# Value bias added to the turned attention output, value copies on ScalarE, gate folding on GpSimd, third batch's norm ahead of the first division

## The reference, cut to what matters

```python
def _L0_attn_ref(x, Wq, bq, Wk, bk, Wv, bv, Wo, bo):
    ...
    V = proj(Wv, bv)
    ...
    att = jax.nn.softmax(scores, axis=-1)
    y = jnp.einsum('bhqk,bhkd->bhqd', att, V)
    y = y.transpose(0, 2, 1, 3).reshape(B, T, H)
    return jnp.einsum('bth,oh->bto', y, Wo) + bo
...
mod = (_silu(L0_c) @ L0_wmod).reshape(L0_c.shape[0], 6, 1, -1)
sa, ca, ga, sb, cb, gb = (mod[:, 0], mod[:, 1], mod[:, 2], mod[:, 3], mod[:, 4], mod[:, 5])
ga = (2 * (ga >= 0) - 1) * jnp.maximum(jnp.abs(ga), 0.25)
gb = (2 * (gb >= 0) - 1) * jnp.maximum(jnp.abs(gb), 0.25)
h = _layernorm(x, axis=-1) * (1 + ca) + sa
x = x + ga * _L0_attn_ref(h, ...)
h = _layernorm(x, axis=-1) * (1 + cb) + sb
x = x + gb * _L0_ffn_ref(h, ...)
```

## Time and profile before

| | us |
|---|---|
| median of 3 runs | 386.95 (384.18 to 386.96) |
| profiled execution, device time | 386.66 |
| its span, first to last instruction | 384.7 |
| TensorE busy | 335.2 (87%) |
| VectorE busy | 282.9 (74%) |
| ScalarE busy | 256.4 (67%) |
| GpSimd busy | 145.7 (38%) |

### The profile page before, as it was taken

How to read it: one execution, slowest core, us unless ns; L and a number is a source line. 1 busy time by engine, 2 the same in 40 slices (tenths; PEclk the granted TensorE clock), 3 DMA queues, 4 the chain that set the end, 5 groups by cost and what they waited for, 6 DMA issues and landing times.

```text
span 384.7 us, 7186 instructions
## 1 busy us (share of the span) xinstructions
PE 335.2 (87%) x2636; PEld 153.8 (40%) x2636; DVE 282.9 (74%) x585; ACT 256.4 (67%) x276; POOL 145.7 (38%) x179
## 2 busy tenths in 40 slices
PE   3759688989899889898999999898998889779996
PEld 3425254546455334334654434335552323141123
DVE  5879968877899986874799877973598467933334
ACT  8580463534289778855488788736678788849980
POOL 6249327601407234941208136722150246212500
PEclk9956899999999999999999999999999999989999
DMA  7335133300026255500144355510060557515540
GB/s 262 113 68 84 26 60 52 47 5 0 4 55 96 79 136 153 164 13 2 29 92 76 86 141 137 132 30 21 13 84 0 136 137 137 107 49 135 158 131 29
DMA packets 27115, 31.53 MB, mean 82 GB/s; under 512 B 6780, under 2 KB 17788, under 8 KB 27068
## 3 DMA queue, kind: packets, MB, share of 16 engines
q1 hardware_dynamic: 23372, 28.57, 32.3%
q0 software_dynamic: 3456, 2.39, 3.0%
q10 hardware_dynamic: 252, 0.11, 0.2%
HBM read 3.57 MB, written 1.05 MB: 12 GB/s over the span
## 4 chain that ended last, share of the span: by engine, by line
PE 51%; DVE 27%; issue 7%; DMA 7%; ACT 4%; SPq 2%; POOL 1%; DVEq 0%; ACTq 0%; POOLq 0%
PE misc L1315 17%; PE big L1315 17%; PE acc L1315 15%; DVE mx L1055 8%; DMA dense<-tp 4%; ACT ring L804 3%; PE misc L1337 2%; DMA block<-qk_turned 1%; DVE xn L995 1%; DMA gm<-wT 1%; SPq L502 1%; DVE second L1140 1%; DVE stats L970 1%; SPq L527 1%; DMA xs<-in_x 1%
## 5 line engine op out<-in xcount | busy, mean ns | idle before, releaser
L804 ACT ACTIVATE ring<-big 128x1024 f32<-128x1024 f32 (+1 forms) x201 | 195.5, 1021 | 79.3 <-PE big L1315 78.4
L1055 DVE TENSOR_REDUCE mx<-misc 128x1 f32<-128x512 f32 (+7 forms) x155 | 87.3, 588 | 23.7 <-PE misc L1315 21.7
L1315 PE MATMUL acc<-ring,cb 128*32 128x512 f32 x512 | 67.8, 604 | 3.1 <-ACT ring L804 1.6
L1315 PE MATMUL big<-tstack,w1s 128*128 128x512 bf16 x192 | 55.0, 381 | 4.0 <-ACT ring L804 3.8
L1315 PE MATMUL misc<-dense,block 128*128 128x320 bf16 (+7 forms) x170 | 43.4, 316 | 11.4 <-DVE mx L1055 10.4
L1315 PE MATMUL big<-dense,block 128*128 128x512 bf16 (+7 forms) x256 | 51.1, 306 | 0.4 <-ACT ring L804 0.2
L1175 DVE SCALAR_TENSOR_TENSOR gm<-acc,cb,gm 128x512 f32<-128x512 f32 (+1 forms) x41 | 30.0, 733 | 25.6 <-PE acc L1315 19.4
L1315 PEld LDWEIGHTS misc<-dense,block 128*128 128x128 bf16 x170 | 20.9, 149 | 51.2 <-DVE mx L1055 41.3
L456 POOL DMA_DIRECT2D block<-qk_turned x66 | 39.3, 601 | 2.5 <-DMA tstack<-tp 1.3
L1315 PE MATMUL acc<-ring,vals 128*32 128x256 f32 (+7 forms) x512 | 37.9, 412 | 0.0
L1315 PEld LDWEIGHTS big<-dense,block 128*128 128x128 bf16 x256 | 28.7, 149 | 22.5 <-ACT ring L804 9.7
(11 more groups left out here) (163 smaller groups left out, 462.8 us busy)
## 6 DMA issues: line engine op xcount, KB each, us to landing
gm<-wT SPq DMA_DIRECT2D x64, 256.0 KB
dense<-qk SPq DMA_DIRECT2D x42, 64.0 KB
tstack<-tp SPq DMA_DIRECT2D x18, 128.0 KB, 4.6
block<-qk_turned POOLq DMA_DIRECT2D x66, 32.0 KB, 3.5
xs<-in_x SPq DMA_DIRECT2D x4, 256.0 KB, 7.8
ca<-in_pack_a SPq DMA_DIRECT2D x1, 769.0 KB, 7.1
out<-lg SPq DMA_DIRECT2D x3, 256.0 KB, 2.3
dense<-tp SPq DMA_DIRECT2D x6, 128.0 KB, 10.4
```

The costliest lines, as they stand in the source:

```text
L804: act.activation(dst, src, func, scale=scale).then_inc(s["ring_read"], 1)
L1055: dve.tensor_reduce(mx[:, g, k:k + n, blk], src, AX.X, ALU.max).then_inc(s["misc_read"], 1)
L1315: return pe.matmul(dst, lhsT, rhs, start=start, stop=stop)
```

## The change

The value bias leaves `values`: it becomes a column of pack_b and is added by `turn_output` when `yT` is copied (a `tensor_scalar` in place of a copy, with a wait for pack_b). pack_a is 128 columns narrower, pack_b one wider. The copies into `vals` for batches 1, 2 and 3 go to ScalarE: for batch 1 behind `take_sums`, for 2 and 3 ahead of the fifth expert unit; VectorE waits there until the bank is read. `fold_gates` goes to GpSimd, behind `stack_q(1)`, with two-operation `tensor_scalar`s and one product per gate. `normalise` of batch 2 stands ahead of that wait and of the first `divide`.

```diff
--- before.py
+++ after.py
@@ -64,9 +64,9 @@
     return out, at
 
 
-A_COLS, A_W = columns(("we", P), ("wd", P), ("wv", D), ("cos", T), ("sin", T), ("be", 1), ("bd", 1), ("bv", D))
+A_COLS, A_W = columns(("we", P), ("wd", P), ("wv", D), ("cos", T), ("sin", T), ("be", 1), ("bd", 1))
 C_COLS, C_W = columns(("cT", NB), ("wmod", 6 * D))
-B_COLS, B_W = columns(("woT", D), ("bout", D), ("wm", D), ("bm", 1), ("emb", D), ("w2", NEP * HR),
+B_COLS, B_W = columns(("woT", D), ("bout", D), ("wm", D), ("bm", 1), ("bv", 1), ("emb", D), ("w2", NEP * HR),
                       ("b2", 2), ("wof", 2 * D), ("bof", D), ("sum", HR), ("first", NE), ("keep", 2))
 
 
@@ -191,7 +191,6 @@
     return uses, banks, previous, [last[1], last[3]]
 
 
-FOLD_AT = [13, 16]
 OPENING, OPENING_BANK, OPENING_PREVIOUS, LAST_IN_ACC = opening()
 
 
@@ -361,7 +360,7 @@
         s = {n: ctx.enter_context(nc.semaphore(n)) for n in (
             "a_loaded", "b_loaded", "c_loaded", "x0_loaded", "x1_loaded", "x_loaded", "w1_loaded", "ones_loaded",
             "nought_ready", "zeroed", "cleared", "k_block_cleared", "spare_cleared", "mod_linked", "marks", "tabled", "shapes_ready", "exp_ready", "abs_ready", "sil_ready", "mod_ready",
-            "gates_filled", "setup_link", "modb_ready", "w1_ready", "summed", "rows_cleared", "tokens_one",
+            "gates_filled", "gates_folded", "setup_link", "modb_ready", "w1_ready", "summed", "rows_cleared", "tokens_one",
             "var_ready", "pow_ready", "xn_ready", "out_gates", "w1_rounded", "w1_less", "expert_gates", "xb_ready", "x1b_ready",
             "misc_filled", "misc_read", "ring_filled", "ring_read", "consumed", "acc_read",
             "qk_ready", "qk_turned", "k_dense_stacked", "q_block0_stacked", "q_block1_stacked", "q_dense_stacked", "k_block_stacked", "nm_ready",
@@ -654,6 +653,14 @@
                 else:
                     pool.tensor_tensor(w1f, rounded, w1f, ALU.add).then_inc(s["w1_less"], 1)
 
+            def fold_gates(k):
+
+                pool.wait_ge(s["abs_ready"], 2 * k + 2)
+                pool.tensor_scalar(graw[k], graw[k], 0.0, 0.5, ALU.is_ge, ALU.subtract).then_inc(s["gates_folded"], 1)
+                pool.tensor_scalar(gabs[k], gabs[k], 0.25, 2.0, ALU.max, ALU.mult).then_inc(s["gates_folded"], 1)
+                pool.wait_ge(s["gates_folded"], 3 * k + 2)
+                pool.tensor_tensor(gate[:, k, :, :], graw[k], gabs[k], ALU.mult).then_inc(s["gates_folded"], 1)
+
             def fold_out(b, here=None):
 
                 if here:
@@ -718,6 +725,8 @@
             cut_weights(0)
             pool.wait_ge(s["spare_cleared"], 2)
             stack_q(1)
+            for k in range(2):
+                fold_gates(k)
             pool.wait_ge(s["qk_turned"], 6)
             stack_k(1)
             k_blocks(1, K_BLOCKS)
@@ -725,7 +734,7 @@
             pool.wait_ge(s["x0_loaded"], 16)
             pool.wait_ge(s["x1_loaded"], 16)
             pool.wait_ge(s["x_loaded"], 16 * (NB - 2))
-            pool.wait_ge(s["gates_filled"], 2)
+            pool.wait_ge(s["gates_folded"], 6)
             fold_out(0)
             pool.wait_ge(s["xb_ready"], 1)
             cut_weights(1)
@@ -827,6 +836,16 @@
                     wait_consumed(act, phase, NSS * g + NSS - 1)
                     act.copy(sums[g][:, :], acc[:, g, :]).then_inc(s["acc_read"], 1)
 
+            def values(here, b, turn=None):
+                wait_softmax_over(act, b, turn)
+                act.wait_ge(s["misc_read"], use_of(here, "v") + CREDIT["misc_read"])
+                wait_filled(act, here, "v")
+                src = bank(here, "v").rearrange("q (s p d) -> q p s d", s=NS, p=NP)
+                for a in range(2):
+                    h = slice(BLK * a, BLK * a + BLK)
+                    ins = act.copy(vals[h, :, :, (HS + 1) * a:(HS + 1) * a + HS], src[h])
+                ins.then_inc(s["misc_read"], 1)
+
             def route(here):
                 wait_read(act, here, "lg")
                 act.activation(ex[:, :, :], lg_of[here[1]], ACT.Exp).then_inc(s["ex_ready"], 1)
@@ -884,13 +903,14 @@
             turn(1)
             softmax(softmax_at(0), {})
             take_sums(softmax_at(0))
+            values(("second", 0), 1)
             for b in range(NB - 2):
                 softmax(softmax_at(None, b), {
                     TURN_AT[0]: lambda: turn(b + 2, [0]), TURN_AT[1]: lambda: turn(b + 2, [1]),
                     TURN_AT[2]: lambda: turn(b + 2, [2]), SUM_AT: lambda: take_sums(softmax_at(None, b), [0]),
                     ROUTE_AT: lambda: route(("loop", b))})
                 change_table(2 * b + 1, ACT.Gelu)
-                experts(b, experts_at(b))
+                experts(b, experts_at(b), {4: lambda: values(("loop", b), b + 2, b)})
                 change_table(2 * b + 2, ACT.Exp)
             softmax(softmax_at(NB - 1), {SUM_AT: lambda: take_sums(softmax_at(NB - 1), [0]),
                                          ROUTE_AT: lambda: route(("late", NB - 2))})
@@ -949,14 +969,6 @@
                 dve.wait_ge(s["cleared"], 2)
                 for a in range(2):
                     link(dve.memset(vals[BLK * a:BLK * a + BLK, :, :, (HS + 1) * a + HS:(HS + 1) * a + HS + 1], 1.0))
-
-            def fold_gates(k):
-
-                dve.wait_ge(s["abs_ready"], 2 * k + 2)
-                link(dve.tensor_scalar(graw[k], graw[k], 0.0, 2.0, ALU.is_ge, ALU.mult))
-                link(dve.tensor_scalar(gabs[k], gabs[k], 0.25, None, ALU.max))
-                link(dve.scalar_tensor_tensor(out=gate[:, k, :, :], in0=graw[k], scalar=-1.0, in1=gabs[k],
-                                              op0=ALU.add, op1=ALU.mult))
 
             def pick_modulation(b, norm):
 
@@ -1034,16 +1046,12 @@
                 cut(rot[:, :], qk, links("rope_link", ROPE_LINKS, b, first=3 if half == 1 else 1), "qk_ready",
                     (0, 1) if half is None else (half,))
 
-            def values(here, b, turn=None):
-                wait_softmax_over(dve, b, turn)
+            def values(here):
                 wait_filled(dve, here, "v")
-                src = bank(here, "v").rearrange("q (s p d) -> q s p d", s=NS, p=NP)
-                bv = A["bv"].rearrange("q (p a d) -> q p a d", p=NP, a=2)
+                src = bank(here, "v").rearrange("q (s p d) -> q p s d", s=NS, p=NP)
                 for a in range(2):
                     h = slice(BLK * a, BLK * a + BLK)
-                    dst = vals[h, :, :, (HS + 1) * a:(HS + 1) * a + HS]
-                    ins = dve.tensor_tensor(dst.rearrange("q p s d -> q s p d"), src[h],
-                                            bv[h, :, a, :].unsqueeze(1).to_broadcast([BLK, NS, NP, HS]), ALU.add)
+                    ins = dve.tensor_copy(vals[h, :, :, (HS + 1) * a:(HS + 1) * a + HS], src[h])
                 ins.then_inc(s["misc_read"], 1)
 
             def maximum(here, g, u):
@@ -1095,7 +1103,8 @@
 
             def turn_output(here):
                 wait_filled(dve, here, "yT")
-                dve.tensor_copy(yT_of[here[1]], bank(here, "yT")).then_inc(s["misc_read"], 1)
+                dve.wait_ge(s["b_loaded"], 16)
+                dve.tensor_scalar(yT_of[here[1]], bank(here, "yT"), B["bv"], None, ALU.add).then_inc(s["misc_read"], 1)
 
             def residual(here):
                 dve.wait_ge(s["xb_ready"], here[1] + 1)
@@ -1233,7 +1242,7 @@
             cut_rotated(0)
             normalise(xs[:, 1], 1, 0, norm_link)
             ones_for_sums()
-            values(here, 0)
+            values(here)
             modulate(0, hT, ahead, "xT", 1)
             wait_read(dve, ahead, "xT")
             dve.wait_ge(s["x_loaded"], 16 * (NB - 2))
@@ -1242,20 +1251,16 @@
             maxima(here, 0, ALONE[:SHIFTED])
             cut_rotated(1)
             maxima(here, 0, ALONE[SHIFTED:])
-            for k, uses in enumerate(WOVEN.values()):
+            for uses in WOVEN.values():
                 for phase, use in uses:
                     if phase == "first":
                         maxima(here, 0, [use])
                     else:
                         maxima(ahead, 1, [use])
-                if k in FOLD_AT:
-                    fold_gates(FOLD_AT.index(k))
-                if k == FOLD_AT[-1]:
-                    dve.sem_inc(s["gates_filled"], 1)
-            values(ahead, 1)
+            normalise(xs[:, 2], 2, 0, norm_link)
+            wait_read(dve, ahead, "v")
             divide(ahead, 0, 0)
             divide(ahead, 0, 1)
-            normalise(xs[:, 2], 2, 0, norm_link)
             maxima(ahead, 1, LEFT)
             for b in range(NB - 2):
                 here = ("loop", b)
@@ -1275,7 +1280,7 @@
                 take_weights(here)
                 if b + 3 < NB:
                     statistics(xs[:, b + 3], b + 3, 2 * b + 4, 0, norm_link)
-                values(here, b + 2, b)
+                wait_read(dve, here, "v")
                 divide(here, b + 1, 1)
                 if b + 3 < NB:
```

(3 more changed lines are left out.)

## The result

The changed kernel takes **382.17 us** (median of 7 runs, 381.69 to 382.61) against 385.42 (384.18 to 386.96) for the kernel before on the same chip: ratio 0.9898, interval 0.9872 to 0.9925. In two later comparisons it took 381.74 against 386.56 (ratio 0.9885, 0.9862 to 0.9909) and 382.00 against 386.68 (0.9893, 0.9854 to 0.9932). All three ratios lie just beyond 1%, but each interval also reaches to less than 1%, and the medians of the first comparison are 3.25 us, 0.8%, apart. One more execution in the second comparison took 471.47 us at a granted clock of 0.661 and is left out of these numbers. I had forecast 383.4 and thought a change within 1% the likelier; the range was 381.9 to 386.2.

A forecast was written before the change was run, and what follows sets the result against it. TensorE and VectorE take turns waiting for each other. Gains of 1.2 + 1.2 + 1.3 - 0.2 = 3.5 us take the profiled 386.66 to 383.2; with the median 0.3 above, 383.4, range 381.9 to 386.2 for 8 in 10.

The forecast's parts named there:

- within 1%: Outcome of neither over 1% faster nor over 1% slower than the kernel before, given a chance of 0.62.
- the price of a GpSimd `tensor_scalar`: Gates on GpSimd: each two-operation instruction taken as 0.6 to 1.3 us, bounded by an `affine_select` of 128 columns at 0.29.
- Part 1: Woven part: moving the gates off VectorE shortens TensorE's waits, gaining 1.2 us, bounds 0.8 and 2.0.
- the slower rival: Near `nm` at 59 us: GpSimd's gates block VectorE, giving 387.1 to 388.6 us; chance 0.07, slower or level.
- the sign I had set for it: Mark of a wrong forecast in the woven part: `nm` above 0.3 us near 59.
- Part 2: End of the opening: norm fits VectorE's wait for `v`, values go to ScalarE; 1.2 us gained, bounds 0.8 and 1.6.
- Part 3: First loop turn: the values leave VectorE, the experts' product starts earlier; 1.3 us gained, bounds 0.8 and 1.66.
- Second turn: Second loop turn: VectorE only waits longer for the weight-spreading DMA; gain 0, bound -0.5.
- `yT`: Copies of `yT`: addition takes 0.75 against 0.68 for the copy, three or four times on the way; -0.2 us.
- The sum's frame: Whole kernel: gains at each place reach the end unless a DMA or third engine comes in; sum 3.5 us.
- the line at 383.1: Whole time below which the kernel counts as over 1% faster, an outcome given a chance of 0.35.

## Why the prediction was right or wrong

Two steps failed: the price of a GpSimd `tensor_scalar`, which took 0.8 us off the gain, and the path behind 334 us, where a wait and the clock behind it gave 2.2 us that the sum didn't have. The rest held.

**Part 1** (1.2 expected, 0.4 measured): the failed step is the price of one `tensor_scalar`, "for four times the columns is at most 1.16": it measured 1.95, 1.5 even with one operation. The bound came from another operation at a quarter of the size, and was none. The mechanism of the slower rival was right, with its place (`nm` near 59) and the time past which it strikes (gates past 58.1), and the sign I had set for it, `nm` above 0.3 us, came (1.40). But I expected its price as one event of 4 us or nothing; it took 1.0 of the 1.4 us that the waits gave back. Those 1.4 are what the woven end wins when nothing holds `nm` (23.65 to 22.24), near my 1.2. And I looked for the hold at the subtraction alone; the cast and `xn`, with one input in SBUF, are held too.

The Trainium skill (SBUF — State Buffer, Who interferes with whom) says more than I used of it: besides two-input instructions it names `cast` and `tensor_scalar` in their fast modes, and says that the later one to issue waits for the whole of the other. The runs agree: the cast at 80.82 took 1.42 for 0.22, `xn` beside a memset that reads nothing 2.49 for 1.11. The Trainium skill (GPSIMD Engine Reference, Engine selection) calls one-input work on GpSimd roughly at line rate; here a one-input instruction of 128x512 took 1.52 and 1.95 us there against 0.42 on VectorE, and more than the 1.28 with two inputs, so the measurement decides against it.

**Part 2** (1.2 expected, 1.55 at LEFT and 1.36 at the `mT` transposes measured, counted from the woven end): right. ScalarE's copies cost 0.62 each, near the 0.58 taken. Two details were wrong: TensorE's wait for the last LEFT maximum went from 1.40 only to 1.22 (I had said 0.2), since its own fills came earlier as well, and `xn` took twice its time, under cover. **Part 3** (1.3 expected): 1.2 from `wT` to `gm1`, with VectorE waiting 0.49 for GpSimd's power as foreseen. **Second turn** 0: right, but by another wait than I said: the one for the DMA stayed (1.67 and 1.70), and a new one of 1.52 for TensorE's `oT` took up what the values had cost. **`yT`** -0.2: right, 0.06 for the first turning and 0.1 from `gm1` to `wT3`. Summed up to `wT3`: 0.4 + 1.4 - 0.06 + 1.2 - 0.1 = 2.8 instead of 3.5; part 1 is 0.8 short, and the small differences of the others nearly cancel.

**The sum's frame** failed at its last step. "Between these places both engines follow each other, so that what is won at one of them reaches the end unless a DMA or a third engine comes in": in the tail a DMA did, and it gave instead of taking. By a sum of 2.8 the span would have come to 381.9; it was 380.3. The three profiled executions of each kernel put 0.7 us on the earlier landing and 1.4 on the clock, and by the mean clocks above the second is in part luck of the draw: the kernel before was profiled three times with the low clock, which a third of its executions seem to lack. In the timed runs this shows as scatter: those of the kernel before run from 384.2 to 387.3 in the second comparison, those of the changed one from 381.4 to 382.9. Lowest against lowest in the three comparisons is 2.5, 2.8 and 2.7, about the place-by-place sum; median against median 3.3 to 4.8. With only the executions of the kernel before whose mean clock is 0.977 or more, the medians of the second and third comparison are 384.73 and 385.12, 3.0 and 3.1 above the changed kernel's.

The sign was right, and "within 1%" was the wrong side to favour: the line at 383.1 lay 0.3 from my forecast, and the term that decided it wasn't in the sum. The 2.8 us that the places gave are 0.7% of the time; what carried the ratio past 1% is the tail, a term that I had at nothing without a reason. That the forecast of 383.4 is only 1.2 us off owes something to chance as well: it started from a median of 386.95, and over seven runs that median was 385.42. The 0.7 us by which my gain was too large hid part of what the high start and the missing tail put on.

## What to carry to other kernels

Before work goes to an idle GpSimd, list the VectorE instructions that lie in SBUF alone and fall beside it or beside whatever it pushes back, not only the gap: here 3.4 us hung on two tiny ones, and halving the block into two gaps was better than either gap. Price an operation on GpSimd only from a row of that operation. A wait for a DMA late in a kernel, with a low clock of TensorE behind it, belongs in the sum as a term with a range of its own: here it was worth up to 2.2 us, and gains there came with work ahead of it that was 2.8 us earlier as well as with work that was 0.6 later. And look at the spread and the clocks of the timed runs before a profile or two are taken for the kernel's own state.

## What the runs showed of the hardware

- GpSimd, 128x512 float32: `tensor_scalar` 1.95 us with two operations, 1.52 with one, product of two tensors 1.28.
- A VectorE cast, subtraction or `tensor_scalar` from SBUF to SBUF ended with the GpSimd instruction beside it (1.42 for 0.22, 2.45 for 0.28, 2.49 for 1.11); three maxima of 320 columns from PSUM took 1.46 us beside the gates' instructions as without them.
- Behind TensorE's waits of 2.3 us and more its granted clock was 0.89 on the mean over 334 to 349 us, and `dense` to end took about 1.4 us longer; behind waits of up to 2.14 it was 1.00.
- ScalarE copied 64x512 from PSUM in 0.62 us, no less than 128x512 (0.58 to 0.59).
